# Batch 1's warp moved into batch 0's attention: taps mixed by GpSimd, projections between the attention steps

## The reference, cut to what matters

```python
x: (2, 1024, 256)                        # batch, rows, columns, f32
w = rigid_transform(x, dx, angle)        # bilinear: four neighbours of a rotated, shifted point
Q, K, V = w @ WQ + bQ, w @ WK + bK, w @ WV + bV       # 16 heads of 16
A = softmax(causal(Q K^T / 4));  x = x + sum_h(A V) @ WO + 16 * bO
y = zX * lap_x(x) + zY * lap_y(x) + zR * x * (1 - x)  # reflecting Laplacian
x = x + sum over the top 2 of 8 experts: w_e * (relu(y @ W1[e] + b1[e]) @ W2[e] + b2[e])
```

## Time and profile before

| | us |
|---|---|
| median of 3 runs | 1067.64 |
| lowest, highest | 1060.93, 1068.91 |
| the profiled execution | 1060.64 |
| its span in the profile | 1058.8 |

### The profile page before, as it was taken

The page is one execution under the profiler, slowest core; times in us unless marked ns, Lnnn a source line. Parts: engine busy times, 40 slices in busy tenths (PEclk is TensorE's granted clock), DMA queues, the critical chain, the costliest instruction groups (busy, mean ns, idle before and its releaser), DMA issues.

```text
span 1058.8 us, 14473 instructions
## 1 busy us (share of the span) xinstructions
PE 729.6 (69%) x4027; PEld 443.1 (42%) x4028; DVE 546.2 (52%) x1095; ACT 358.0 (34%) x915; POOL 219.0 (21%) x232
## 2 busy tenths in 40 slices
PE   0450122821238599999999884806999999999993
PEld 0340111411114244444446342703677677677662
DVE  6174565575776478877787741641233232332330
ACT  0122333312222366666574563000322322322320
POOL 0114464143421000000200023150211211221121
PEclk9865555955558799999999997757999999999997
DMA  7689896988617507754621052841122122122123
GB/s 252 211 255 317 286 320 211 354 246 303 222 80 238 121 3 221 222 142 132 218 81 51 33 195 91 272 144 36 30 35 35 30 35 35 30 35 35 30 29 91
DMA packets 95522, 150.99 MB, mean 143 GB/s; under 512 B 9365, under 2 KB 69322, under 8 KB 95306
## 3 DMA queue, kind: packets, MB, share of 16 engines
q1 hardware_dynamic: 74136, 85.76, 26.2%
q0 software_dynamic: 16784, 61.51, 19.4%
q10 hardware_dynamic: 4546, 3.08, 1.0%
HBM read 95.86 MB, written 56.37 MB: 144 GB/s over the span
## 4 chain that ended last, share of the span: by engine, by line
PE 53%; issue 13%; DVE 13%; DMA 10%; SPq 4%; ACT 3%; POOL 2%; ACTq 0%; POOLq 0%; DVEq 0%
PE psum L1206 13%; PE psum L1190 13%; PE psum L1127 6%; PE psum L966 5%; PE psum L1141 4%; DMA arena<-table,tap_col 3%; PE psum L1198 3%; DVE arena L1504 3%; SPq L562 2%; PE psum L1090 2%; ACT arena L900 2%; SPq L518 2%; DVE arena L1445 1%; DMA table<-arena 1%; DMA qk_rows<-arena 1%
## 5 line engine op out<-in xcount | busy, mean ns | idle before, releaser
L900 ACT ACTIVATE arena<-psum 128x512 f32<-128x512 f32 (+3 forms) x384 | 170.6, 490 | 139.2 <-PE psum L1146 92.7
L1504 DVE TENSOR_REDUCE arena<-psum 128x2 f32<-128x1024 f32 (+3 forms) x168 | 155.1, 953 | 58.3 <-PE psum L972 47.2
L947 ACT ACTIVATE arena<-psum,b_cols 128x128 f32<-128x128 f32 x312 | 84.9, 383 | 262.7 <-PE psum L1198 262.7
L1206 PE MATMUL psum<-arena 128*128 x624 | 142.7, 382 | 3.1 <-ACT arena L947 3.1
L1190 PE MATMUL psum<-arena 128*128 x312 | 142.3, 599 | 0.8 <-DVE arena L1676 0.7
L1141 PE MATMUL psum<-arena 99*128 99x512 bf16 (+3 forms) x384 | 109.7, 331 | 25.5 <-DMA arena<-arena 12.2
L1016 PE MATMUL psum<-cst,arena 128*128 128x128 f32 x32 | 10.9, 445 | 168.6 <-DVE arena L1451 168.6
L1206 PEld LDWEIGHTS psum<-arena 128*128 128x128 f32 x624 | 116.7, 192 | 18.4 <-issue 3.8
L966 PE MATMUL psum<-arena 96*128 96x512 bf16 (+4 forms) x384 | 110.2, 356 | 12.1 <-DVE arena L1504 12.0
L818 POOL DMA_INDIRECT results<-arena,home x39 | 60.7, 1555 | 269.6 <-DVE arena L1695 211.4
L1684 DVE COPY arena<-psum 128x1024 f32<-128x1024 f32 x39 | 47.7, 1224 | 101.7 <-PE psum L1190 101.7
(11 more groups left out here) (170 smaller groups left out, 927.9 us busy)
## 6 DMA issues: line engine op xcount, KB each, us to landing
pairs_x<-zeros SPq DMA_DIRECT2D x4, 4160.0 KB, 20.0
arena<-L_ffn_W SPq DMA_DIRECT2D x16, 1024.0 KB
arena<-qk_rows SPq DMA_DIRECT2D x16, 768.0 KB
table<-arena SPq DMA_DIRECT2D x20, 384.0 KB
qk_rows<-arena SPq DMA_DIRECT2D x16, 384.0 KB, 3.3
arena<-pairs_x SPq DMA_DIRECT2D x39, 130.0 KB, 2.0
qk_rows<-arena SPq DMA_DIRECT2D x16, 256.0 KB, 3.4
padded<-arena SPq DMA_DIRECT2D x2, 1328.0 KB
```

The costliest lines, as they stand in the source:

```text
L900: nc.scalar.activation(probs[at % 2][h][:, q0:512], banks[turn % SCORE_BANKS][:, q0:512], ACT.Exp, scale=DH ** -0.5).then_inc(exp_done, 1)
L947: ins = nc.scalar.activation(hidden_t[:, f], banks[3 + f // 4][:, (f % 4) * P:(f % 4 + 1) * P], ACT.Relu, bias=b1_cols[:, bass.ds(e, 1), f])
L1206: ins = t_.matmul(banks[5][:, 0:D], hidden_t[:, f], w2_all[:, bass.ds(e, 1), f].squeeze(1), start=f == 0, stop=f == FC - 1)
L1504: v.reduce_max(part[:, 2 * pair:2 * pair + 2, qb], psum[:, at:at + 2, 0:keys], AX_X).then_inc(max_read, 1)
```

## The change

Batch 1's taps and projection leave the stages ahead of attention. `warp_stages` now ends with the projection of batch 0 and the four rounds of maxima. What is left of batch 1 is spread over the attention groups 0 to 3:

- GpSimd gathers a block (`gather`, four indirect transfers, two blocks in flight at most) and mixes it (`mix`: six operations on 128x768, two on 128x256). It copies V of groups 0 and 1 behind its second block, and V of group 2 behind its sixth.
- ScalarE makes the hats: block 0 behind the projection, blocks 1 and 2 ahead of the first exponential, blocks 3 to 7 in four parts of two activations in the steps of `HATS_AT`. It also takes over the clearing of `v_group` and the rows of ones in the stacks.
- TensorE turns block k at step `TURN_AT[k]`, projects Q and K at `PROJECT_AT` and V at `VALUES_AT`, all as side uses; VectorE reads them. GpSimd makes the second and third parts of batch 1's chunks.
- All pairs of group 4 stand in steps 3 to 10 of group 3, three a step, and its turn_max in step 11. Group 2 loses eight early pairs; group 4 gets eight more, those of group 5.
- The chunks are taken in another order (`chunk_place`): the first four chunks hold the heads of two groups, so stacks 0 and 1 are loaded when four chunks are stored, and the others are stored behind that.
- SyncE's list: `store_neg(3)` stands behind the stores of batch 1's first four chunks; the loads of stacks 4 and 5, the other chunks, x1 and `clear_pairs(0)` follow; `clear_pairs(1)` follows `store_neg(4)`; the last two follow the load of stack 7. Batch 1's taps use x1's buffer, so x1 is loaded after the last block is turned.

The steep case (rotation beyond the shear) is also moved; it is chosen by a value at run time.

```diff
+ALL_PAIRS = [(pair, r) for r in (0, 7, 1, 5, 4, 2, 6, 9, 8, 3, 10, 11) for pair in range(2)]
+HATS_AT = {3: (0, 2), 4: (0, 6), 5: (0, 10), 6: (1, 2), 7: (1, 8)}
+TURN_AT = [(0, 1), (0, 2), (0, 4), (0, 9), (1, 2), (1, 8), (2, 2), (2, 8)]
+PROJECT_AT = [(2, 8), (2, 9), (2, 10), (2, 11), (3, 0), (3, 0), (3, 1), (3, 1)]
+VALUES_AT = [(3, 2), (3, 2), (3, 3), (3, 3)]
+FIRST_OF_NEXT = (3, 3)
...
+def chunk_place(j):
+    return j // 2 % 2, j // 4, j % 2          # kind, c, half; before: j // 4, j // 2 % 2, j % 2
...
-            with eng.Fori(SB // 2, SB) as it:
-                yield "taps", 1, it
-                yield "maxima", 0, it - SB // 2
-            yield "project", 1
+            with eng.Fori(0, HG) as it:
+                yield "maxima", 0, it
...
 # SyncE, stage "project" of batch 0
+                    store_parts(b, range(PART_SLOTS))
+                    parts_are_stored(b, 0)
+                    for g in range(2):
+                        load_stack(g, g)
+                    store_parts(b, range(PART_SLOTS, QK_CHUNKS))
+                    parts_are_stored(b, 1)
+                    for g in range(2, NG):
+                        load_stack(g, g)
...
 # SyncE, attention
+            for g in range(NG - 1):
+                store_neg(g, g)
+            store_parts(1, range(PART_SLOTS))
+            store_neg(NG - 1, NG - 1)
+            parts_are_stored(1, 0)
+            for g in range(2):
+                sp.wait_ge(pv_done, (g + 1) * NS)
+                load_stack(g + NG, g)
+            store_parts(1, range(PART_SLOTS, QK_CHUNKS))
+            sp.wait_ge(max_read, USE_OF["turn_w", SB - 1, 1] + 1 + 2)
+            (load of x1)
+            clear_pairs(0)
+            parts_are_stored(1, 1)
+            sp.wait_ge(pv_done, (NG - 1) * NS)
+            load_stack(2 * NG - 2, NG - 2)
             store_neg(NG, 0)
+            clear_pairs(1)
             sp.wait_ge(pv_done, NG * NS)
             load_stack(2 * NG - 1, NG - 1)
+            clear_pairs(2)
             clear_pairs(NG - 1)
...
 # GpSimd
+            def mix(k):
+                u = k % 2
+                steps = Steps(pool, late_steps, k * MIX_STEPS)
+                t = late_taps[u]
+                pool.wait_ge(late_hats_steps, (k + 1) * 8)
+                for d in range(3):
+                    steps.mark(g_.tensor_tensor(t[d], t[d], late_hats[u][0][:, d:d + 1].broadcast_to([P, 3, D]),
+                                                ALU.mult))
+                steps.wait()
+                for d in (1, 2):
+                    steps.do(g_.tensor_tensor(t[0], t[0], t[d], ALU.add))
+                steps.do(g_.tensor_tensor(t[0], t[0], late_hats[u][1], ALU.mult))
+                steps.do(g_.tensor_tensor(t[0][:, 0], t[0][:, 0], t[0][:, 1], ALU.add))
+                if k >= 2:
+                    pool.wait_ge(max_read, USE_OF["turn_w", k - 2, 1] + 1 + 2)
+                steps.do(g_.tensor_tensor(late_warped[u], t[0][:, 0], t[0][:, 2], ALU.add))
+                g_.sem_inc(late_mixed, 1)
...
+                        while ahead < min(k + 2 if k else 1, SB):
+                            if ahead == 1:
+                                for u in range(PART_SLOTS):
+                                    pool.wait_ge(parts_stored[u], PART_STORES * 2)
+                            gather(ahead)
+                            ahead += 1
+                        pool.wait_ge(late_taps_in[k % 2], 48 * (k // 2 + 1))
...
+                    mix(k)
+                    if k == 1:
+                        group_of_v(0)
+                        group_of_v(1)
+                    if k == 5:
+                        group_of_v(2)
```

More of the change, by code:

```diff
@@ L506, in _, with store_parts @@
         def _(sp):
-            def store_parts(b):
-                for j in range(QK_CHUNKS):
-                    kind, c, half = j // (2 * DC), j // 2 % DC, j % 2
+            def store_parts(b, chunks):
+                for j in chunks:
+                    kind, c, half = chunk_place(j)
                     sp.wait_ge(parts_ready, b * QK_CHUNKS + j + 1)
@@ new lines, in _ @@
+            for u in range(2):
+                pool.wait_ge(strip_stored[u], 48 * (JB + 1))
+            pool.wait_ge(index_ready, NB + 1)
+            steep_1 = pool.value_load(steep[0:1, SB:SB + 1], min_val=0, max_val=1)
+            with pool.If(steep_1 < 1):
+                second_batch(True)
+            with pool.If(steep_1 > 0):
+                second_batch(False)
+            pool.wait_ge(late_mixed, SB)
+            g_.memset(v_all[:, 1, :, :, DH:DH + 1], 1.0).then_inc(v_cleared, 1)
@@ L786, in sideways @@
+            group_of_v(NG - 1)
+            for j in range(QK_CHUNKS):
+                pool.wait_ge(max_read, USE_OF["project", j, 1] + 1 + 2)
+                g_.tensor_copy(parts[j % PART_SLOTS][:, 1], resid[j % 2]).then_inc(halved, 1)
+                pool.wait_ge(halved, QK_CHUNKS + j + 1)
+                g_.tensor_tensor(parts[j % PART_SLOTS][:, 2], resid[j % 2], parts[j % PART_SLOTS][:, 1],
+                                 ALU.subtract).then_inc(parts_ready, 1)
             def sideways(b):
@@ L1058, in read @@
                     pe.wait_ge(max_read, USE_OF[what_, i_, b] + 1 + 2)
-                if what == "pair":
+                if what == "turn_w":
+                    pe.wait_ge(late_mixed, i + 1)
+                    for c in range(DC):
+                        ins = t_.transpose(bank[:, c * P:(c + 1) * P], late_warped[i % 2][:, c * P:(c + 1) * P], ident)
+                elif what == "project":
+                    pe.wait_ge(max_read, USE_OF["turn_w", SB - 1, 1] + 1 + 2)
+                    ins = project_qk(bank, m, i)
+                elif what == "values":
+                    ins = project_v(bank, m, i)
+                elif what == "pair":
+                    if m not in stacks_read:
+                        pe.wait_ge(stack_in[m % NG], STACK_IN * (m // NG + 1))
+                        stacks_read.append(m)
                     pair, r = i
```

286 lines of the change are left out of this document (202 added, 84 removed).

## The result

The changed kernel takes 1049.52 us in the median (1047.84 to 1051.46, 4 runs); the kernel before took 1065.63 in the same series. The ratio is 0.986, with an interval of 0.983 to 0.989: faster by 1.4 per cent, where the forecast had said 5.6 per cent. The time lies above the range of 988 to 1043. The profiled execution has a span of 1049.6 and 1051.46 in all.

What follows compares the result with a forecast made beforehand. A slack, serial stage before attention (gathers, VectorE's mixing, projection, maxima), then full groups paced by TensorE and VectorE. Gain 100, less 20 and 7.2 growth and 16.5 waits: -56.3, span 1002.5, median forecast 1008 us; range 988 to 1043.

Steps and rivals of the forecast that it cites:

- waits for `turn_w`: TensorE's waits for mixed blocks 2 to 7 in the groups: short, 3 us together.
- GpSimd's pace: Gathering and mixing batch 1's blocks during attention: 15.9 us a block, giving short waits of 3 us together.
- Rival 1: GpSimd moderately slower under contention: 23 us a block, each us over 16 costing 6, total 1015 to 1046; chance 16%.
- gain of 100: Stage between batch 0's projection and attention: attention starts at about 255 us instead of 355.1.
- Path A: Start of attention: group 0's maxima, through stacks, scores, negating and SP's queue, land near 250 to 255 us.
- Path B: Start of attention: GpSimd gathers and mixes blocks 0 and 1, then copies V, ready at 257 us.
- price of 0.9 us a pair: Attention groups: each pair more in a step costs 0.9 us.
- Group 4's +7.2: Group 4 has three pairs in its first eight steps and grows by 7.2 us.
- credit of 7.2 for eight pairs: Group 2 loses eight pairs, saving 7.2 us against 7.1 for four added projections.
- The waits at the ends of groups 2 and 3: TensorE waits for the next group's maxima: 9 us ahead of group 3, 4.5 ahead of group 4.
- rival 2: SP's first-in, first-out queue delays store_neg(5); groups 4 and 5 wait 7 and 20 us, total 1016 to 1035; chance 12%.
- Contention: GpSimd and VectorE sharing SBUF in attention: VectorE mostly reads PSUM, so the uncontended price of 1.03 us was taken.

Runs made afterwards that it cites:

- e1: Changed kernel with the six large operations of GpSimd's mix on 24 elements instead of 768: 1011.6 us, ratio 0.962 to the kernel before.
- e4: Changed kernel with ScalarE's hats and TensorE's turns of blocks 2 to 7 placed one to three steps later: 1016.1 us, ratio 0.967 to the kernel before.
- c2_four: Changed kernel with the edits of e3, e7 and e8 and the later places of e4: 1000.7 us, ratio 0.950 to the kernel before.
- e7: Changed kernel with block 1 mixed by VectorE instead of GpSimd: 1041.0 us, ratio 0.977 to the kernel before.
- e8: Changed kernel with group 0's negated rows stored ahead of stacks 2 and 3 in SyncE's list: 1039.5 us, ratio 0.974 to the kernel before.
- e3: Changed kernel with group 3's negated rows stored ahead of batch 1's first four chunks in SyncE's list: 1026.3 us, ratio 0.977 to the kernel before.
- d1: e3's kernel with one of two products over the feature halves in batch 1's Q and K chunks: 1021.7 us, ratio 0.972 to the kernel before.

## Why the prediction was wrong

The sum of the prediction, step by step, against the profile of the kernel after (borders as in the windows above):

| step | forecast | measured | difference |
|---|---|---|---|
| first score | 255 | 260.1 | +5.1 |
| group 0 | 43 | 54.3 | +11.3 |
| group 1 | 34 | 52.0 | +18.0 |
| waits for `turn_w` | 3 | in the groups | -3.0 |
| group 2 with the wait at its end | 35 + 9 | 47.1 | +3.1 |
| group 3 with the wait at its end | 49 + 4.5 | 59.1 | +5.6 |
| group 4 to the end | 570.0 | 577.1 | +7.1 |
| span | 1002.5 | 1049.6 | +47.1 |

**The step that failed is "GpSimd's pace"**, in its size and in its form. It had 15.9 us a block, and "short waits, 3 us together". The pace was 18.2, 2.3 more: 1.9 are the mix, whose operations on 768 took 1.81 us and those on 256 0.72 instead of 0.55, and the rest stands around the gather. The price of 1.56 was the 1.03 of 508 elements scaled by length, 2.03 ns an element, and the mix needed 2.36. The operation on 508 still took 1.03 in the kernel after, so the row was read rightly but was of a cheaper kind of operation; no run shows why. The form was worse: I looked for its effect only in TensorE's wait for a mixed block, and that was indeed 3.7 us. I had not asked who else waits in order for what GpSimd issues. ScalarE's hats wait for fractions which GpSimd gathers only behind the mix of two blocks earlier; the exponentials stand behind the hats, TensorE's products behind the exponentials, and GpSimd in turn waited for the hats of block 7 (kernel after, waits of GpSimd):

```profile
POOL arena L881 <- ACT arena L1009: 6.8, 1, 6.8
```

That GpSimd's mix is the cause is shown: e1 takes its operations away and gets back 25.9 of the some 29 us that groups 0 and 1 were over the forecast. That in-order waits for it are a part is shown too: e4 moves only the places and gets back 10.8. The rest is not divided by any run; the hold on VectorE has a share in it (5.7 us in one place in e4_later, 5.3 in c2_four), and that was a term which the prediction put at nothing.

Rival 1 named this engine, with 23 us a block and "each us over 16 costs 6". At the measured 18.2 its rule gives 14 us; the two groups cost twice that. It was the right engine, but too cheap, since ScalarE's wait was missing there too.

**The clock.** The forecast kept it at 1.0 in the groups. Waits of a few us in TensorE were followed by stretches at half clock: 0.50 over 326 to 332, a mean of 0.80 in group 1. In e1_mix_short, where the waits are gone, it is 1.00. So a wait in these groups costs more than its own length. How much of the 29 us is this, no run separates.

**Start of attention.** The gain of 100 was 95. Path A's 250 to 255 was 260.0: the transfer of the negated rows took 15 us, against 8.9 before, issued at 346.19 and used at 355.13. Path B's first product at 260 was 265.7: the gather landed 7 us late and the mix was 1.9 longer. That both would end together was right, and it is why e1 and e7, which undo only path B, did nothing at the start. e8 undoes path A, and failed because the mix of block 1 then held VectorE's negating; with both edits the start came 10 us earlier.

**Pairs and projections.** In sum +8.7 for groups 2 and 3, of which I can place a part. The price of 0.9 us a pair was read from the 40.9 of group 0, which hold the start of attention as well: from product to product group 0 is 37.5 long and group 1 33.4, or 0.5 a pair. Group 4's +7.2 came true in this kernel (47.1 for 39.9), but it was 5.6 in six of the others (45.5), so the hit is partly luck. A chunk took 1.95 us and a piece of V 1.93 instead of 1.8: 12 x 0.14 = 1.7. Seven of the eight chunks, not four, fall ahead of group 3's first product with V, which only moves length from group 3 to group 2. Of the credit of 7.2 for eight pairs, 5.1 came: without its chunks (7 x 1.95 = 13.7) e3's stretch of 21.4 would be 7.7, against 12.8 before. This is an estimate that takes each chunk at its full time, which d1 shows to be too much. The first seven steps, where one block is turned, took 25.0 against 20.6 before; I had 0.5 for a turn. And the last three steps of group 3 took 17.0 us in e3 against 7.4 before. There 24 pairs in eight steps end late on VectorE, the maxima are read and turned behind them, TensorE waits, and its clock falls (0.51 in the last step). Timelines of VectorE and TensorE, e3_neg_first:

```profile
459.13 0.19 DVE L1699 TENSOR_TENSOR arena<-arena 128x32 f32<-128x32 f32 x1
```

```profile
459.69 0.27 PE L1278 MATMUL psum<-cst,arena 128*32 128x128 f32 x1 [1.90 <-DVE arena L1700]
464.55 0.61 PE L1353 MATMUL psum<-arena 99*128 99x512 bf16 x1 [2.91 <-DMA arena<-arena]
```

This part was read, not tested.

**The waits at the ends of groups 2 and 3** were right in cause and near in size: 7.8 for 9, and 3.2 for 4.5; e3 shows the first. **The two rivals on transfers:** SyncE's queue (rival 2) did not come about, since the rows for group 5 were issued at 515.16, 6.9 us ahead of the group's first score (522.02), which waited for nothing. **Contention** I had set aside, since "VectorE mostly reads PSUM". The rows of e8 and of the kernel after show that its few small operations between two SBUF regions are held, one of them 3.08 us long instead of 0.19, and in e4_later and c2_four one 5.66 and 5.31 instead of 0.23, with TensorE behind it. This is what the Trainium skill says in SBUF — State Buffer, Who interferes with whom: the port pair that the two engines share is an exclusive lock, and the second one blocks until the first is done. I had weighed only the milder sentence of another page. The trace agrees with the lock, but the longest holds here lasted over three operations in a row, not only until the one under way was done. It agrees, too, with the page's remark that a GpSimd operation which only writes does not hold a VectorE operation with two inputs (0.19 beside the memsets).

**Group 4 to the end.** Of the 7.1 us, 1.9 are only the border: the forecast's 570.0 begin at 496.2, 1.9 us behind group 4's first score. Another 2.4 lie between that score and the first product with V (6.0 us, at a mean clock of 0.69, against 3.5 before), and 2.9 behind group 4, half of them in group 7: 37.4 us before and 38.9 after. Group 7 is long in both kernels, and 24.4 in e4_later, in whose series the kernel before had a median of 1050. Windows of the kernel after, then of e4_later:

```profile
606.90:645.80 38.90, 26.60 (x175) 8.85 (x174) 7.68 (x31) 19.04 (x44) 15.62 (x16) 0.78 0.45 161
```

```profile
593.80:618.20 24.40, 21.57 (x172) 7.75 (x172) 7.68 (x31) 18.49 (x44) 14.34 (x15) 1.00 0.68 246
```

It is a stall beside the indirect transfers that goes with the series, not with the change, as the fourteen profiles above show; no run settles its cause.

## What to carry to other kernels

When work moves onto a slow engine inside a full stage, don't ask only who consumes its result: list every engine that waits in program order for anything it issues, small gathers included, and place those waits a step or more behind its real pace. Look also at what the slow engine's operations hold on its neighbour, and for how many of them in a row. Where two paths end together, undoing one may show nothing; price and test them together. And treat a wait inside a stage where TensorE is full as dearer than its length, where the profile shows the clock falling behind it, as here.

## What the runs showed that I had not expected

- GpSimd's TensorTensor took 1.81 us on 768 elements, 0.72 on 256 and 0.23 on 24: 2.1 ns an element and 0.18 fixed. Broadcast operands and broken pieces cost nothing on top: with and without a broadcast it was 1.81, and the 256 in one piece lie on the line through the 24 and 768 in three. Not every form lies on it: 508 elements took 1.03, and 512 with bf16 out 1.16. The Trainium skill, GPSIMD Engine Reference, Performance versus the Vector engine, has 4497 ns for 2048 elements, 2.2 ns each: this agrees, and was the better estimate than my row.
- One VectorE operation of 0.19 us took 3.08 beside it, and one of 0.23 took 5.31 and 5.66, up to three whole operations of GpSimd (1.81 each) in a row.
- The negated rows, three issues of 1.9 us in all, took 15.1 us to their use where two gathers and two stacks filled the DMA engines, and 8.9 before. In e8_neg0_first, where the stacks stood behind them, it was 3.3 (255.98 to 259.29).
